# Listing and running the full halves of an expert's rows before a chunk's groups are complete, in three larger chunks

## The reference, cut to what matters

```python
x = x + tanh(g_xattn) * xattn(ctx, layernorm(x))      # q, k, v, softmax, @ Wo + bo
h = layernorm(x)
probs = softmax(h @ Wr + br)                          # 8 experts
top_p, top_i = top_k(probs, 2)
cw = sum(one_hot(top_i, 8) * top_p[..., None], -2)
y[e] = relu(h @ W1[e] + b1[e]) @ W2[e] + b2[e]        # 128 -> 256 -> 128
x = x + tanh(g_ffn) * sum_e(cw[e] * y[e])
```

## Time and profile before

| | |
|---|---|
| median of 3 runs | 797.29 us (795.64 to 798.03) |
| profiled execution | 798.88 us, its span 797.2 us |
| TensorE busy | 769.3 us (97%) |
| TensorE weight loads busy | 647.4 us (81%) |
| VectorE, ScalarE, GpSimd busy | 525.8, 495.1, 427.6 us |
| DMA, mean | 146 GB/s |

### The profile page before, as it was taken

How to read it: one execution, slowest core, us unless ns; L and a number is a source line. 1 busy time by engine, 2 the same in 40 slices (tenths; PEclk the granted TensorE clock), 3 DMA queues, 4 the chain that set the end, 5 groups by cost and what they waited for, 6 DMA issues and landing times.

```text
span 797.2 us, 17389 instructions
## 1 busy us (share of the span) xinstructions
PE 769.3 (97%) x5426; PEld 647.4 (81%) x5426; DVE 525.8 (66%) x1820; ACT 495.1 (62%) x1623; POOL 427.6 (54%) x439
## 2 busy tenths in 40 slices
PE   7999999999999999999999999999999999989997
PEld 6778777776889888778988778898877898878775
DVE  5646667595857567677758777766768556566444
ACT  4776677776866566767556576656667665563332
POOL 2233365656542435785655686665568566424551
PEclk9999999999999999999999999999999999999999
DMA  7835152542545532174664136565315556533221
GB/s 197 234 126 192 60 213 87 192 149 78 169 167 181 190 138 71 51 225 159 217 213 125 57 100 216 187 209 182 109 48 169 177 172 204 191 106 90 57 80 54
DMA packets 115069, 116.39 MB, mean 146 GB/s; under 512 B 13961, under 2 KB 90530, under 8 KB 114978
## 3 DMA queue, kind: packets, MB, share of 16 engines
q1 hardware_dynamic: 106880, 100.44, 38.2%
q0 software_dynamic: 7168, 14.69, 6.3%
q10 hardware_dynamic: 930, 0.15, 0.1%
HBM read 34.44 MB, written 40.04 MB: 93 GB/s over the span
## 4 chain that ended last, share of the span: by engine, by line
PE 80%; POOL 5%; issue 5%; DVE 4%; ACT 4%; DMA 1%; SPq 1%; ACTq 0%; DVEq 0%; POOLq 0%
PE shared L1449 13%; PE batch L1387 11%; PE batch L1400 11%; PE hid_ps L1310 8%; PE xy_ps L1324 7%; PE batch L1395 6%; PE batch L1377 3%; PE shared L1233 3%; PE shared L1235 3%; PE shared L1234 3%; ACT probs L757 3%; POOL probs L687 2%; PE xy_ps L1287 2%; POOL yg L677 2%; PE shared L1359 2%
## 5 line engine op out<-in xcount | busy, mean ns | idle before, releaser
L687 POOL TENSOR_TENSOR probs<-probs,rsums 128x512 f32<-128x512 f32 x128 | 132.9, 1038 | 233.0 <-DVE rsums L1163 231.4
L757 ACT ACTIVATE probs<-batch,neg_max 128x128 f32<-128x128 f32 x512 | 180.5, 374 | 2.0 <-DVE neg_max L1167 2.0
L838 ACT ACTIVATE qT<-shared,tb 128x512 f32<-128x512 f32 x128 | 87.2, 696 | 85.6 <-PE shared L1235 74.3
L1400 PE MATMUL batch<-pT_sb,kvn 128*128 128x512 f32 x256 | 133.6, 603 | 2.9 <-ACT pT_sb L765 2.9
L1387 PE MATMUL batch<-kvT,qT 128*128 128x128 f32 x1024 | 135.4, 275 | 0.8 <-ACT qT L838 0.8
L662 POOL DMA_INDIRECT sorted_x<-xn,row_of x112 | 115.3, 1029 | 26.7 <-issue 26.6
L1449 PE MATMUL shared<-M,oT 128*128 128x128 f32 x1024 | 125.5, 276 | 0.3
L1387 PEld LDWEIGHTS batch<-kvT,qT 128*128 128x128 f32 x1024 | 124.4, 192 | 1.2 <-ACT qT L838 1.2
L1449 PEld LDWEIGHTS shared<-M,oT 128*128 128x128 f32 x1024 | 119.4, 192 | 1.7 <-issue 1.6
L757 ACT ACTIVATION_READ_ACCUMULATOR probs<-batch,neg_max 128x1 f32 x512 | 110.2, 215 | 0.0
L1163 DVE RECIPROCAL rsums<-sums 128x4 f32<-128x4 f32 x128 | 22.7, 177 | 131.5 <-ACT probs L757 115.4
(11 more groups left out here) (177 smaller groups left out, 1250.0 us busy)
## 6 DMA issues: line engine op xcount, KB each, us to landing
wt<-wall SPq DMA_DIRECT2D x124, 321.0 KB
sorted_x<-yg SPq DMA_DIRECT2D x36, 512.0 KB, 5.0
xt<-sorted_x SPq DMA_DIRECT2D x147, 64.0 KB
sorted_y<-y_sb SPq DMA_DIRECT2D x71, 128.0 KB
kv<-in_ctx_dram SPq DMA_DIRECT2D x16, 256.0 KB
kv<-in_x_dram SPq DMA_DIRECT2D x16, 256.0 KB
xres<-in_x_dram SPq DMA_DIRECT2D x32, 128.0 KB
out_dram<-x SPq DMA_DIRECT2D x15, 256.0 KB
```

The costliest lines, as they stand in the source:

```text
L687: nc.gpsimd.tensor_tensor(pv, pv, rsums[:, m % 2, :].unsqueeze(2).broadcast_to([P, 4, P]), ALU.mult).then_inc(probs_ready, 1)
L757: last = nc.scalar.activation(probs[:, m % 2, c * P:(c + 1) * P], batch_ps[m % BANKS][:, c * P:(c + 1) * P], ACT.Exp, bias=neg_max[:, m % ...
L838: nc.scalar.activation(qT[:, g % 2, :, number, :], sh[:, :].rearrange("p (b i) -> p b i", b=GB), ACT.Identity, bias=tb[:, number:number + ...
L1400: nc.tensor.matmul(batch_ps[m % BANKS][:, :], kvn[:, m % KVN, :], pT_sb[:, :], start=True, stop=True).then_inc(o_ready, 1)
```

## The change

- The chunks are 5, 5 and 4 groups, each with a DRAM tensor of its own (`sorted_rows`), never used twice.
- Inside a chunk there are several lists (`LISTS`): after three, four and all five groups (three and four in the last chunk). An early list holds only halves that are already full, and of those as many as the worst case guarantees (17 and 25 halves); the last one holds the rest. Tiles of a list start by the same rule as before, 8 (g + 2) + 11. `list_halves` carries on from list to list what is new for each expert, and `open_list` (VectorE, slot 8 (g + 2) + 4, three small instructions) prepares the next.
- The number of halves is the same worst case of the larger chunks: 47, 47 and 39 in 24, 24 and 20 tiles.
- Outputs of a half are written over its rows (two transfers for a tile of two halves, by register addresses), so a row's outputs lie at the row: `find_homes`, `home` and `row_at` go, and gathers use `row_of`.
- Gathers of a chunk start when its last tile is stored, in slots 73, 113 and 143 and later; three are allowed in each of the last eight dense steps (151 to 158). Groups 12 and 13 both have `SUMMED` 158.
- 63 fills of 512 KB, spread over slots 1 to 56 (slots 1, 9, 17, 25, 33, 41 and 49 have two), in runs of 2 KB in place of 4 KB.

By the code's constants tiles stand in slots 43-54, 59-70, 83-94, 99-110, 123-142, where before they stood in 43-58, 67-82, 91-106 and 115-142. Lists fall on slots 33, 41, 49, 73, 81, 89, 113 and 121, before on 33, 57, 81, 105 and 121. Up to slot 130 the gathers fill slots 73 to 129 but for 111 and 112, by the same rule of slots as before. `LATE_GROUP`, from which gathers have two more buffers, is 7 in place of 9. The dense steps are in slots 143 to 158 in both.

```diff
-CHUNKS = (3, 3, 3, 3, 2)
+CHUNKS = (5, 5, 4)
...
+LISTED = ((3, 4, 5), (3, 4, 5), (3, 4))
+
+
+def full_halves(k, m):
+
+    return HALVES[k] if m == CHUNKS[k] else (2 * m * TOK - E * (HALF - 1) + HALF - 1) // HALF
+
+
+LISTS = tuple((k, FIRST_GROUP[k] + m - 1, full_halves(k, m)) for k in range(NCH) for m in LISTED[k])
+N_LISTS = len(LISTS)
+LIST_AT = {g: v for v, (_, g, _) in enumerate(LISTS)}
+
+
+def opens(v):
+
+    return v == 0 or LISTS[v][0] != LISTS[v - 1][0]
+
+
+def closes(v):
+
+    return v + 1 == N_LISTS or LISTS[v][0] != LISTS[v + 1][0]
+
+
+TILES_TO = tuple(FIRST_TILE[k] + (TILES[k] if g == LAST_GROUP[k] else upto // 2) for k, g, upto in LISTS)
+LIST_OF_TILE = tuple(min(v for v in range(N_LISTS) if i < TILES_TO[v]) for i in range(N_TILES))
...
+FILLS = [(k, e, j) for k in range(NCH) for j in range(max(CHUNKS)) for e in ((E, 0, 2, 4, 6) if j == 0 else (0, 2, 4, 6))]
+CLEARING = 56
...
-    for k in range(NCH):
-        n = max(n, GB * (LAST_GROUP[k] + 2) + 7 + AHEAD)
-        for _ in range(TILES[k]):
+    for v, (_, g, _) in enumerate(LISTS):
+        n = max(n, GB * (g + 2) + 7 + AHEAD)
+        for _ in range(LISTED_FROM[v], LISTED_FROM[v + 1]):
...
-                    room = 2 if n in DENSE_AT else 1
+                    room = 2 + (n >= DENSE_SLOT[E]) if n in DENSE_AT else 1
...
-        summed.append(n + LANDED if n + LANDED < DENSE_SLOT[0] else min(n + 2, DENSE_SLOT[-1]))
+        summed.append(n + LANDED if n + LANDED < DENSE_SLOT[0] else max(n, min(n + 2, DENSE_SLOT[-1])))
...
-        xs = [nc.dram_tensor(f"sorted_x{p}", (E * ROWS, D), F32).ap() for p in range(SETS)]
-        ys = [nc.dram_tensor(f"sorted_y{p}", (max(TILES) * TILE, D), F32).ap() for p in range(SETS)]
+        sorted_rows = [nc.dram_tensor(f"sorted{k}", (E * ROWS + SPARE, D), F32).ap() for k in range(NCH)]
...
-                p, q = q // FILLS, q % FILLS
-                sp.dma_start(xs[p][q * FILL:(q + 1) * FILL, :].rearrange("(p r) d -> p (r d)", p=P), zeros[:, :]).then_inc(cleared[p], 16)
+                k, e, j = FILLS[q]
+                if e < E:
+                    rows_of = sorted_rows[k][0:E * ROWS, :].rearrange("(e r) d -> e r d", e=E)[e:e + 2, j * TOK:(j + 1) * TOK, :]
+                    rows_of = rows_of.rearrange("e (p r) d -> p e (r d)", p=P)
+                else:
+                    rows_of = sorted_rows[k][E * ROWS:E * ROWS + SPARE, :].rearrange("(e p r) d -> p e (r d)", e=2, p=P)
+                sp.dma_start(rows_of, zeros.rearrange("p (e n) -> p e n", e=2)).then_inc(cleared[group_cleared(k, j)], 16)
...
             def load_tile(i):
-                k = CHUNK_OF_TILE[i]
-                t = i - FIRST_TILE[k]
-                if t == 0:
-                    wait_shared(sp, shared_out, "table", LAST_GROUP[k], 0)
-                    wait_rows_scattered(sp, k)
-                if t % AT_ONCE == 0:
-                    read_table(mybir.EngineType.SP, 0, first_rows, i, N_TILES, E * ROWS - HALF)
+                if opens_list(i):
+                    g = LISTS[LIST_OF_TILE[i]][1]
+                    wait_shared(sp, shared_out, "table", g, 0)
+                    wait_rows_scattered(sp, g)
+                if reads_table(i):
+                    read_table(mybir.EngineType.SP, 0, first_rows, i, N_TILES, E * ROWS + SPARE - HALF)
                 wait(sp, xt_ready, i - XB + 1)
                 for a in range(PARTS[i]):
-                    sp.dma_start(xt[:, i % XB, a, :], xs[k % SETS][bass.ds(first_rows[i, a], HALF), :]).then_inc(got_x[i % XB], 16)
+                    sp.dma_start(xt[:, i % XB, a, :], sorted_rows[CHUNK_OF_TILE[i]][bass.ds(first_rows[i, a], HALF), :]).then_inc(got_x[i % XB], 16)
...
             def store_tile(i):
-                k = CHUNK_OF_TILE[i]
-                t = i - FIRST_TILE[k]
-                if t == 0 and k >= SETS:
-                    wait_outputs_gathered(sp, k - SETS)
                 wait(sp, y_done, i + 1)
-                rows_of = ys[k % SETS][t * TILE:t * TILE + PARTS[i] * HALF, :]
-                sp.dma_start(rows_of.rearrange("(a p) d -> p a d", p=HALF), y_sb[:, i % 2, 0:PARTS[i], :]).then_inc(y_stored[i % 2], 16)
+                for a in range(PARTS[i]):
+                    sp.dma_start(sorted_rows[CHUNK_OF_TILE[i]][bass.ds(first_rows.pop((i, a)), HALF), :], y_sb[:, i % 2, a, :]).then_inc(y_stored[i % 2], 16)
...
-                nc.gpsimd.indirect_dma_start(outputs_of(g)[:, c, choice, :], None, ys[k % SETS][0:HALVES[k] * HALF, :],
-                                             bass.IndirectOffsetOnAxis(ap=home[:, g, choice, c:c + 1], axis=0)
+                nc.gpsimd.indirect_dma_start(outputs_of(g)[:, c, choice, :], None, sorted_rows[k][:, :],
+                                             bass.IndirectOffsetOnAxis(ap=row_of[:, g, choice, c:c + 1], axis=0)
                                              ).then_inc(gathered[BUFFER[g]], 16)
...
+            def list_halves(n, s):
+                if s == 1 and g in LIST_AT:
+                    v = LIST_AT[g]
+                    k = LISTS[v][0]
+                    nth = v - min(u for u in range(N_LISTS) if LISTS[u][0] == k)
+                    now, kind = nth % 2, 0 if opens(v) else 2 if closes(v) else 1
+                    mine, next_ = (0 if nth == 0 else 1 + nth % 2), 1 + (nth + 1) % 2
+                    cols = 2 + E if closes(v) else 1 + E
+                    new = n_halves[:, now, :] if opens(v) else n_new[:, :]
+                    nc.vector.scalar_tensor_tensor(out=filled[:, :, :], in0=next_row[:, :].unsqueeze(2).broadcast_to([P, E, J]),
+                                                   scalar=0.0 if closes(v) else 1.0 - HALF, in1=begins[:, :, :],
+                                                   op0=ALU.add, op1=ALU.is_gt).then_inc(table_step, 1)
+                    dve.wait_ge(table_step, TABLE * v + 1)
+                    nc.vector.tensor_reduce(n_halves[:, now, :], filled[:, :, :], AX, ALU.add).then_inc(table_step, 1)
+                    dve.wait_ge(table_step, TABLE * v + 2)
+                    if opens(v):
+                        nc.vector.scalar_tensor_tensor(out=adds[:, mine, 0, 2:2 + E], in0=n_halves[:, now, :], scalar=-float(HALF),
+                                                       in1=leap[:, kind, :], op0=ALU.mult, op1=ALU.add).then_inc(table_step, 2)
+                    else:
+                        nc.vector.tensor_tensor(n_new[:, :], n_halves[:, now, :], n_halves[:, 1 - now, :], ALU.subtract).then_inc(table_step, 1)
+                        nc.vector.scalar_tensor_tensor(out=adds[:, mine, 0, 2:2 + E], in0=n_halves[:, now, :], scalar=-float(HALF),
+                                                       in1=leap[:, kind, :], op0=ALU.mult, op1=ALU.add).then_inc(table_step, 1)
+                        dve.wait_ge(table_step, TABLE * v + 3)
+                    nc.vector.tensor_tensor(n_upto[:, :, :], before[:, 1:E + 1, :], new.unsqueeze(1).broadcast_to([P, E, E]),
+                    dve.wait_ge(table_step, TABLE * v + 5)
+                    nc.vector.tensor_reduce(ends[:, 2:2 + E], n_upto[:, :, :], AX, ALU.add).then_inc(table_step, 1)
+                    dve.wait_ge(table_step, TABLE * v + 6)
+                    past = tile_id if opens(v) else since
+                    nc.vector.scalar_tensor_tensor(out=hit[:, :, 0:cols], in0=ends[:, 0:cols].unsqueeze(1).broadcast_to([P, 2, cols]),
+                                                   scalar=past[:, 0:1], in1=adds[:, mine, :, 0:cols],
+                                                   op0=ALU.is_lt, op1=ALU.mult).then_inc(table_step, 1)
+                    dve.wait_ge(table_step, TABLE * v + 7)
+                    nc.vector.tensor_reduce(adds[:, next_, :, 0] if not closes(v) else found[:, :], hit[:, :, 0:cols], AX,
+                                            ALU.add).then_inc(table_step, 1)
...
+            def open_list(n, s):
+                if s == 4 and g in LIST_AT and not closes(LIST_AT[g]):
+                    v = LIST_AT[g]
+                    nth = v - min(u for u in range(N_LISTS) if LISTS[u][0] == LISTS[v][0])
+                    now, mine, next_ = nth % 2, (0 if nth == 0 else 1 + nth % 2), 1 + (nth + 1) % 2
+                    past = tile_id if opens(v) else since
+                    dve.wait_ge(table_step, TABLE * (v + 1))
+                    nc.vector.tensor_tensor(since[:, :], past[:, :], ends[:, 1 + E:2 + E], ALU.subtract)
+                    nc.vector.tensor_scalar(leap[:, 2 if closes(v + 1) else 1, 0:E - 1], n_halves[:, now, 1:E], float(HALF), float(ROWS),
+                                            ALU.mult, ALU.add)
+                    nc.vector.scalar_tensor_tensor(out=adds[:, next_, 0, 1:2], in0=n_halves[:, now, 0:1], scalar=float(HALF),
+                                                   in1=adds[:, mine, 0, 1 + E:2 + E], op0=ALU.mult, op1=ALU.add).then_inc(list_opened, 1)
```

196 lines of the change are left out of this document (84 added, 112 removed).

## The result

The changed kernel takes 802.92 us, median of twelve runs (799.63 to 805.60), and the kernel before 797.34 in the same comparison: a ratio of 1.0069 [1.0053, 1.0085]. It is slower by 5.6 us where 4.6 us faster was forecast. In a comparison on a second chip the ratio was 1.0147 [1.0129, 1.0165], on a third 1.0061 [1.0039, 1.0083]; the experiments come to that. The profiled execution has a span of 799.2 us and took 800.92 at a mean granted clock of 0.995, near the fast end of the twelve; the runs at 0.991 took 803.3 to 805.6.

What follows compares the result with a forecast made beforehand. TensorE, busy 769.3 of 797.2 us, was taken as the bound. Fifteen halves fewer (-15.0) and the other terms summed to -4.6 us: span 792.6, profiled time 794.3, median 792.7 us, range 788.0 to 797.5.

Steps and rivals of the forecast that it cites:

- Points 1 to 5: Before slot 127: fewer halves -15.0 us, lost idle filling +2.4, slots 120-122 +2.0, gathers 0, lists +2.3, find_homes gone -0.7.
- Point 9: Fills and stores on SP: two fills make the first tile's weights late once, +1.0 us, between 0 and 3.
- Point 10: Row addresses, start-up work and SP's waits for scatters at lists: nothing, up to +1 us each in slots 47 and 87.
- slower rival: "The fills starve the tiles": slots 43 to 56, twelve tiles each wait 1.0 us for weights, 803.7 us; chance 0.09.
- Point 7: At the end: groups 12 and 13 both summed at 158, two more combines of 1.04 us, +2.1 us.
- Point 8: Slots 151 to 158: three gathers a step, GpSimd falls behind 0.25 us a step; +0.3 us, between 0 and 3.
- point 6: Slot 130 holds two halves where before it held one: +1.0 us.
- GpSimd's gathers end the kernel: Rival, dense steps: GpSimd loses 0.42 us a step, last gather and end 1.2 us later, 793.9 us; chance 0.10.

Runs made afterwards that it cites:

- best version: Changed kernel with 48-word table rows, fills in slots 1 to 36, gathers moved in slots 128 to 142, three a dense step from 151: 789.61 us, 0.9912 of before.
- first profile: The changed kernel's profiled execution in the first comparison: span 799.2 us, time 800.92; that comparison's ratio to the kernel before was 1.0069.
- fifth set: On another chip with stalls, changed kernel with only its gathers moved in slots 128 to 142: 1.0079 of before; with fills in slots 1 to 36 too: 1.0033.
- second profile: The changed kernel run again unaltered, on a second chip, where the dense steps stall: 1.0147 of the kernel before.
- three repairs: Changed kernel with table rows of 48 words for 47, fills in slots 1 to 36, and late gathers moved: 0.9915 and 0.9912 of before without stalls.
- few gathers in a row: Changed kernel, 48-word rows, early fills, one gather in slots 128 to 130, two from 138 to 142, three every third dense step: 0.9915; with stalls 0.9955.
- third set: Chip without dense-step stalls: changed kernel 1.0061 of before; with rows, fills and gathers edited 0.9915 and 0.9912; kernel before, three gathers a step plus memsets, 0.9968.

## Why the prediction was wrong

The forecast was a span of 792.6 us and 794.3 for the profiled execution, and 792.7 for the median. The profiled execution has 799.2 and 800.92, the median is 802.92. Of the 10.2 us, 6.6 are in the span and 3.6 between that execution and the median.

- *Points 1 to 5, right as a sum.* With the weights in time the 52 tiles end 9.9 us earlier than before and, in the best version, which still waits 1.09 us in slot 98, 10.4; forecast 9.0. Slots 120 to 123 take 17.1 us (17.9), slots 72 to 79 36.4 and slots 112 to 119 37.8 (36 to 37); the wait for the table without a tile is 0.78.
- *Point 9, the step that failed.* It had the weights late once, for 1.0 us (0 to 3). They were late four times, 2.13 + 2.00 + 1.16 + 1.20 = 6.5 us. For the one place that it had, slot 43 behind two fills, the price of 1.0 was half of what the trace shows, 2.13 us, and inside its bounds; the other profiles with both fills there have 0.95 to 2.25. By ring order, the rule of the Trainium skill quoted in the prediction (DMA: Bandwidth & Descriptors, Queues, rings and completion order), it would be 2.0, and the trace comes near it. What was missing is that the wait repeats, and why: SP's own loads from the table. Point 10 went through what SP does and left its register loads out; they take 1.1 us more each in the median, up to 3.8, ahead of tile weights. Each of the two edits shows one side of it: without fills beside the tiles slot 127 starts 6.6 us ahead of the 681.5 of the first profile, with quick loads 4.0, both on another chip; within the fifth set the early fills bring 4.9. The share of the DMA engines wasn't it, for in slots 48 to 55 it is 0.64 and the prediction had 0.86. The slower rival had the mechanism and 12 tiles at 1.0 us; four tiles paid 1.6.
- *Point 7, right.* +2.1 against two blocks of 1.04 in the trace. *Point 8*: 0.60 us of waiting for 0.3. But that GpSimd "falls behind" was priced only as its own lateness. In four of the five sets the others wait for it too: in the second profile of the changed kernel ScalarE starts the last dense step 55.7 us behind the first, in the first profile 51.1.
- *The tile slots from 127 on*, priced by point 6 alone. TensorE waits 0.62, 1.68 and 3.19 us there; before 2.07 at the last of these places and under 0.2 at the others. Five gathers in slots 128 and 129 beside the tiles' transfers and ScalarE's loads of 2.5 us (0.98 before, 1.07 in the best version) are what the best version changes, and its waits are 0.98 and 1.25. The last wait goes with the loads: the profiles with rows of 47 words have 2.90 to 3.52 us there, those of the fifth set with their gathers moved too, and those with rows of 48 words 1.25 to 2.24; the versions that put two gathers in every other slot from 132 stand apart, with 5.70 and 4.37. How the rest of the 4.6 us splits wasn't tried on a chip without stalls.
- *The clock*, not in the sum at all. The runs of the changed kernel have 0.989 to 0.995 and follow it by 0.9 us a thousandth; those of before have 0.997 in the median. Some of the low figure is free: behind TensorE's last matmul at 790.9 the clock is 0.70, which is 0.003 of the mean (before 0.89, which is 0.001). The 2.0 us from the profile (0.995) to the median (0.993) go with the rest. What brings them stays open: the kernel before, with four stalls in its dense steps, had 0.998 in its profiled execution, and the best version 0.9955 in the median, with few waits.

The ranking of the rivals was wrong in one way: "GpSimd's gathers end the kernel" and "fills starve the tiles" were taken as excluding each other, and parts of both came, with a third cause that no rival had.

## What to carry to other kernels

A layout that shrinks a table can slow the instruction that reads it into registers: look at the duration of every load, not at the diff, and keep rows at a multiple of 16 bytes. A queue that issues fills, register loads and weights in one order has to be priced with all three, at each slot in which they meet. Denser gathers on GpSimd are not only GpSimd's own time: put fewer of them in a step than fill it, and measure on more than one chip, for here the same program stalls on some and not on others. With the three repairs the change is worth 0.9% (0.9912 and 0.9915); on the chip with stalls 0.45% with few gathers in a row, and 0.1%, at the edge of the noise, with three a step from 151. And when gathers are moved, look at what their sums do at the end: here they moved too, and paid part of the gain.

## What the runs showed of the hardware

- A register load from a table in SBUF: 0.53 to 0.66 us in the median from rows of 128 or 48 words, 1.68 from rows of 47 or 129, up to 3.8; of the two lists of the changed kernel that start at a multiple of 16 bytes, list 4 is read in 0.53 and 0.54, and list 0 in 0.53 to 1.66, much as in the kernel before (0.52 to 1.33); lists 2 and 6, which start at a multiple of 8 bytes, are as slow as the rest (1.47 to 2.87). The Trainium skill (DMA: Bandwidth & Descriptors, Latency and other measured facts) gives about 600 ns as the floor of `tensor_load`; the quick ones agree with it in size, though the quickest here took 0.27.
- In four sets of runs TensorE's signals reached ScalarE, VectorE and GpSimd up to 5 us late while GpSimd issued gathers back to back, and came in a bunch 1 to 2 us after the last gather. TensorE's matmuls are recorded on time meanwhile. The third set and the changed kernel's first profile show none of it in the dense steps. What differs between the chips is open, and so is whether the signals or the matmuls' ends are late, since these ends are modelled.
